# The last step of a layer norm moves from VectorE to ScalarE in an adjacency-attention kernel

## The chip, the cores and the metric

The kernel runs on one core of a Trainium2 chip. The metric is the device time of one launch in microseconds (us). Engine names in the profile: PE is TensorE, with PEld for its weight loads; DVE is VectorE; ACT is ScalarE; POOL is GpSimd; SP is SyncE, which issues the DMAs here. Each engine executes its own instructions strictly in the order in which the kernel lists them, and the engines are tied together by semaphores: an instruction may increment one when it has ended, and another engine waits for a value of it.

## What is computed

For each of 16 batches, with x of 1024 x 512 and an adjacency matrix of 1024 x 1024 that all batches share:

```python
q = jnp.einsum('bnd,ed->bne', neuron_states, Wq)
k = jnp.einsum('bnd,ed->bne', neuron_states, Wk)
v = jnp.einsum('bnd,ed->bne', neuron_states, Wv)
rel = jnp.einsum('bnd,bmd->bnm', q, k)
rel = adjacency.T[None, :, :] * rel
rel = rel / jnp.linalg.norm(rel, axis=2, keepdims=True)
return jnp.einsum('bnm,bmd->bnd', rel, v)
...
x = _layernorm(x + _L0_gnn_ref(x, adj, L0_gnn_Wq, L0_gnn_Wk, L0_gnn_Wv), axis=-1)
```

The layer norm is `(x - m) / sqrt(v + eps)`, with mean and variance over the 512 columns of a row, and no learned scale or bias.

## The kernel before

Every matrix product is made in three matmuls of split operands: each fp32 operand is split into a high part (a copy by ScalarE into a shorter format, names ending in `_hi`) and a low part (the difference, by VectorE or GpSimd, names ending in `_lo`), and `product` adds high by high, high by low and low by high (lines 339, 340 and 341). The products of the y and s stages are made by a Strassen-like scheme with seven products of blocks in place of eight.

A batch runs through four stages on TensorE, without a pause in between by its program:

- y stage (`y_products`): the batch's x by the combined weights. It makes 14 products of 6 matmuls in the order of `Y_ROUNDS` = 1, 5, 2, 6, 4, 7, 3, each round for j = 0 and 1. Round 2 adds onto the bank that round 1 filled, and so waits for `y_p1`, ScalarE's copy of round 1's result (line 495, the first thing that ScalarE does in a batch, for j = 0 and 1). Round 1 and round 5 make 24 matmuls together.
- s stage (`s_products`, two pairs of row blocks): 28 products that make `rel`. VectorE and GpSimd add the blocks and multiply them by the adjacency (line 669 is the first on VectorE), ScalarE squares them (line 534), GpSimd adds the squares (line 833) for the norm.
- v stage (`v_products`): eight products of 12 matmuls.
- output stage (`outputs`): eight tiles t of 128 rows, 24 matmuls each, into bank t. Tile t needs chunk t, the high and low parts of the 128 columns of `rel` that belong to it (`chunk_hi` by ScalarE, line 543; `chunk_lo` by VectorE, line 705). There are three chunk buffers (`CRING`), so chunk t+3 is made when tile t is done.

While TensorE makes the output tiles, the helpers do three things at once. For each t in turn, in this order:

- ScalarE makes `x_hi` of the next batch's x pieces (line 463; two pieces at t=0 and t=1, one at t=2 to 5, none at 6 and 7), then `chunk_hi` of t+3 once tile t is done. Nothing else stands in ScalarE's list there.
- VectorE makes `x_lo` of the same pieces (line 582, waits for `x_hi`), then `output(t)`: the sum of the scaled tile and the residual x (line 728), its statistics (731), mean and variance (733), and variance plus epsilon (735); then `chunk_lo` of t+3; then it waits for GpSimd's `rstd` and makes `normalise(t)` in place in `res`, tile (t mod 4) of a ring of four (line 740).
- GpSimd makes the sums of x pieces that the Strassen scheme wants (lines 780 to 792), S1 and S3 ahead of the first `power_var`, S2 ahead of the second, S4 ahead of the third; `power_var(t)` raises variance plus epsilon to the power -1/2 (line 850).
- SP stores tile t when `normed` counts it, and loads the residual for the ring's next use behind it (line 268). After the eighth tile it goes on to the next batch's four adjacency blocks (line 261).

At the end of the eight tiles every engine goes to the y stage of the next batch. The last batch has no next x to prepare. The first batch's x is prepared before the loop.

Of the kernel before, what the change touches and what calls it, by code (L numbers as in the profile page):

```python
# [5 lines left out]
F32 = mybir.dt.float32  # L6

F32R = mybir.dt.float32r
ALU = mybir.AluOpType
ACT = mybir.ActivationFunctionType  # L10
AX = mybir.AxisListType

P = 128
# [17 lines left out]
def adjacency_attention_layernorm(nc, x, xT, adj, wq, wk, wvT, a_kept, w_kept, out):  # L31
# [9 lines left out]
    MT = N // P  # L41
# [10 lines left out]
    RRING = 4  # L52

    with ExitStack() as ctx:
        def sb(name, shape, dt):
            return ctx.enter_context(nc.sbuf_tensor(name, shape, dt))

        def sem(name):
            return ctx.enter_context(nc.semaphore(name))
# [9 lines left out]
        res = sb("res", [P, RRING, D], F32)  # L69
# [7 lines left out]
        mean_var = sb("mean_var", [P, 2], F32)  # L77
        var_eps = sb("var_eps", [P, 1], F32)
        rstd = sb("rstd", [P, 1], F32)

        bank = [ctx.enter_context(nc.psum_tensor(f"bank{i}", [P, BANK], F32)) for i in range(8)]

# [65 lines left out]
        mean_var_made = sem("mean_var_made")  # L148
        var_made = sem("var_made")
        rstd_made = sem("rstd_made")  # L150
        normed = sem("normed")


# [53 lines left out]
        def v_bank(m):  # L207
            return bank[(2 + m) % 8]
# [44 lines left out]
        def cols(i):  # L253
            return slice(i * P, (i + 1) * P)
# [200 lines left out]
        def _(act):  # L455
            def x_piece(b, q):
                if q in (X22, X12):
                    act.wait_ge(x_loaded[1], b * DMA + DMA)
                elif q in (X21, X11):
                    act.wait_ge(x_loaded[0], b * DMA + DMA)  # L460
                else:
                    act.wait_ge(x_sum, b * 4 + x_sum_place[q])
                act.activation(x_hi[:, q, :, :], raw_of[q], ACT.Copy).then_inc(x_hi_made, 1)
# [28 lines left out]
            def y_blocks(b):  # L492
                for j in range(2):
                    act.wait_ge(y_done, y_count(b, 1, j))
                    act.activation(y_p1_raw[j], y_bank["a"][j][:], ACT.Copy).then_inc(y_p1, 1)
                for j in range(2):
                    act.wait_ge(y_done, y_count(b, 2, j))
                    act.activation(y_c11_raw[j], y_bank["a"][j][:], ACT.Copy).then_inc(y_c11, 1)
                    y_hi_piece(b, B11, j, y_bank["a"][j][:])
                for j in range(2):  # L500
                    act.wait_ge(y_done, y_count(b, 4, j))
                    y_hi_piece(b, T3, j, y_bank["b"][j][:])
                for j in range(2):
                    act.wait_ge(y_t2, b * 2 + (j + 1))
                    y_hi_piece(b, T2, j, y_t2_raw[j])
                for j in range(2):
                    act.wait_ge(y_c22, b * 2 + (j + 1))
                    y_hi_piece(b, B22, j, y_b22_raw[j])
                for j in range(2):
                    act.wait_ge(y_t1, b * 2 + (j + 1))  # L510
                    y_hi_piece(b, T1, j, y_t1_raw[j])
                    act.wait_ge(y_c12, b * 2 + (j + 1))
                    y_hi_piece(b, B21, j, y_b21_raw[j])

            def y_last_block(b):
                for j in range(2):
                    act.wait_ge(y_t4, b * 2 + (j + 1))
                    y_hi_piece(b, T4, j, y_t4_raw[j])

            def s_copy(b, i):  # L520
                act.wait_ge(s_done, s_count(b, 1, i))
                act.activation(c21(i), s_bank[i // 2]["a"][i % 2][:], ACT.Copy).then_inc(s_p1, 1)  # L522

            def square(b, name, i):
                act.wait_ge(masked_sem[name], b * HT + (i + 1))
                if (name, i) in firsts:

                    act.wait_ge(blocks_turned, b * HALVES + (half_of[name] + 1))
                    target = square_sum[:, half_of[name], :]
                else:  # L530
                    n = added_order.index((name, i))
                    act.wait_ge(square_added, b * ADDED + (n + 1))
                    target = squares[:, n % SQRING, :]
                act.activation(target, block_of[name](i), ACT.Square).then_inc(squared, 1)  # L534

            def chunk(b, t):
                if t < CRING:
                    act.wait_ge(s_done, b * S_COUNT + S_COUNT)
                    for masked in (s_m11, s_m22, s_m21, s_m12):
                        act.wait_ge(masked, b * HT + HT)  # L540
                else:
                    act.wait_ge(o_done, b * MT + (t - CRING + 1))
                act.activation(chunk_hi[t % CRING], rel[:, :, cols(t)], ACT.Copy).then_inc(chunk_hi_made, 1)  # L543

            def v_piece(b, m):
                act.wait_ge(v_done, b * MT + (m + 1))
                act.activation(v_hi[:, m, :], v_bank(m)[:], ACT.Copy).then_inc(v_hi_made, 1)

            def batch(b, last):
                y_blocks(b)  # L550
                s_copy(b, 0)
                s_copy(b, 1)
                y_last_block(b)
                for name, i in square_order[0:6]:
                    square(b, name, i)
                s_copy(b, 2)
                s_copy(b, 3)
                for name, i in square_order[6:]:
                    square(b, name, i)
                for m in range(MT):  # L560
                    v_piece(b, m)
                    if m in (1, 2):
                        chunk(b, m - 1)
                chunk(b, 2)
                if not last:
                    act.wait_ge(v_done, b * MT + MT)
                for t in range(MT):
                    if not last:
                        for q in {0: (X22, X21), 1: (X11, X12), 2: (S1,), 3: (S3,), 4: (S2,), 5: (S4,)}.get(t, ()):
                            x_piece(b + 1, q)  # L570
                    if t + CRING < MT:
                        chunk(b, t + CRING)

            with act.Fori(0, B - 1) as b:
                batch(b, False)
# [3 lines left out]
        def _(dve):  # L579
            def x_piece(b, q):  # L580
                dve.wait_ge(x_hi_made, b * 8 + x_place[q])
                dve.tensor_tensor(x_lo[:, q, :, :], raw_of[q], x_hi[:, q, :, :].bitcast(F32),  # L582
                                  ALU.subtract).then_inc(x_split, 1)
# [114 lines left out]
            def v_piece(b, m):  # L698
                dve.wait_ge(v_hi_made, b * MT + (m + 1))
                dve.tensor_tensor(v_lo[:, m, :], v_bank(m)[:], v_hi[:, m, :].bitcast(F32),  # L700
                                  ALU.subtract).then_inc(v_split, 1)

            def chunk(b, t):
                dve.wait_ge(chunk_hi_made, b * MT + (t + 1))
                dve.tensor_tensor(chunk_lo[t % CRING], rel[:, :, cols(t)], chunk_hi[t % CRING].bitcast(F32),
                                  ALU.subtract).then_inc(chunk_split, 1)
# [27 lines left out]
                dve.wait_ge(mean_var_made, b * MT + (t + 1))  # L734
                dve.tensor_scalar(var_eps[:, :], mean_var[:, 1:2], EPS, None, ALU.add).then_inc(var_made, 1)  # L735

            def normalise(b, t):
                slot = t % RRING
                dve.wait_ge(rstd_made, b * MT + (t + 1))
                dve.tensor_scalar(res[:, slot, :], res[:, slot, :], mean_var[:, 0:1], rstd[:, 0:1],  # L740
                                  ALU.subtract, ALU.mult).then_inc(normed, 1)

            def batch(b, last):
                y_blocks(b)
                s_blocks(b, 0)
                s_blocks(b, 1)
                for m in range(MT):
                    v_piece(b, m)
                    if m in (1, 2):
                        chunk(b, m - 1)  # L750
                    if m == 3:
                        norms(b)
                chunk(b, 2)
                for t in range(MT):
                    if not last:
                        for q in {0: (X22, X21), 1: (X11, X12), 2: (S1,), 3: (S3,), 4: (S2,), 5: (S4,)}.get(t, ()):
                            x_piece(b + 1, q)
                    output(b, t)
                    if t + CRING < MT:
                        chunk(b, t + CRING)  # L760
                    normalise(b, t)

            with dve.Fori(0, B - 1) as b:
                batch(b, False)
# [3 lines left out]
        def _(pool):  # L768
# [78 lines left out]

            def power_var(b, t):
                pool.wait_ge(var_made, b * MT + (t + 1))
                pool.tensor_tensor(rstd[:, :], var_eps[:, :], minus_half[:, 0:1], ALU.pow).then_inc(rstd_made, 1)  # L850

            def batch(b, last):
# [43 lines left out]
```

## Time and profile before

| | |
|---|---|
| median of 3 runs | 2037.12 us (2036.22 to 2037.63) |
| the profiled execution | 2035.14 us, its span 2033.0 us |
| PE, busy share of the span | 98% |
| PEld | 80% |
| DVE | 73% |
| POOL | 46% |
| ACT | 34% |
| line 740 (normalise), DVE | 128 instructions, 100.9 us, mean 788 ns |
| its idle time before, ended by line 850 on POOL | 102.7 us, 128 times |
| mean granted TensorE clock | 0.994 |

The span runs from the first to the last instruction; the rest of the profiled execution's time lies around it. Busy shares are means over the whole span and over stages with different limits. Matmuls are pipelined: each is shown with about 0.39 us, and in an undisturbed stretch one starts every 0.227 us. In the timelines the time in brackets is the engine's idle time before the instruction and the work that ended it.

### The profile page before, as it was taken

The numbers are of one execution on the slowest core, as the hardware profiler recorded it, in microseconds if no ns is written. First come the engines' busy times: TensorE is split into PE (matmuls) and PEld (weight loads), VectorE is DVE, ScalarE is ACT, GpSimd is POOL, SyncE is SP. The second block draws the span as 40 slices with busy tenths as digits, with TensorE's granted clock in tenths as the row PEclk, the third lists the DMA queues.
The fourth block names the chain that finished last, engine by engine and source line by source line (L and its number), as shares of the span: only waits on it lengthen the run. The fifth ranks groups of instructions, "written<-read, shape, count | busy, mean of one in ns | idle before, by whom it ended". The sixth has DMA issues, their size and how long they took to land.

```text
span 2033.0 us, 26047 instructions
## 1 busy us (share of the span) xinstructions
PE 1983.2 (98%) x8688; PEld 1631.2 (80%) x8688; DVE 1484.1 (73%) x2199; ACT 701.2 (34%) x1016; POOL 927.2 (46%) x629
## 2 busy tenths in 40 slices
PE   4999999999999999999999999999999999999998
PEld 3787887878878787887878878788787888878787
DVE  6777777776777677676777777777787677767765
ACT  5342423333233332333423234242333323333331
POOL 2643437344363453535535364353734536355351
PEclk7999999999999999999999999999999999999999
DMA  6344342334333334233342424333333332333401
GB/s 240 122 161 139 139 140 103 129 132 157 124 118 126 132 139 160 83 143 115 150 150 101 155 87 157 139 149 130 113 124 134 150 132 111 129 129 139 160 21 62
DMA packets 70443, 265.44 MB, mean 131 GB/s; under 512 B 7328, under 2 KB 7328, under 8 KB 66208
## 3 DMA queue, kind: packets, MB, share of 16 engines
q1 hardware_dynamic: 70432, 265.32, 35.9%
q8 instruction: 4, 0.07, 0.0%
q14 instruction: 7, 0.06, 0.0%
HBM read 225.97 MB, written 39.32 MB: 130 GB/s over the span
## 4 chain that ended last, share of the span: by engine, by line
PE 87%; DVE 8%; ACT 2%; issue 2%; DMA 0%; SPq 0%; DVEq 0%; POOLq 0%; POOL 0%; ACTq 0%
PE bank L339 29%; PE bank L341 29%; PE bank L340 29%; DVE yv L619 5%; ACT yv L490 2%; DVE rel L640 1%; DVE rel L654 0%; DVE rel L647 0%; DMA scr<-xT 0%; DVE x_lo L582 0%; ACT rel L522 0%; DVE aw L605 0%; DVE rel L598 0%; DVE rel L595 0%; DVE rel L596 0%
## 5 line engine op out<-in xcount | busy, mean ns | idle before, releaser
L339 PE MATMUL bank<-yv 128*128 128x512 f32 x1024 | 398.3, 389 | 0.0
L340 PE MATMUL bank<-yv 128*128 128x512 f32 x1024 | 398.3, 389 | 0.0
L341 PE MATMUL bank<-yv 128*128 128x512 f32 x1024 | 398.3, 389 | 0.0
L339 PE MATMUL bank<-yv,x_hi 128*128 128x512 f32 x896 | 351.5, 392 | 18.5 <-DVE yv L619 16.8
L833 POOL TENSOR_TENSOR square_sum<-square_sum,squares 128x512 f32<-128x512 f32 x224 | 319.2, 1425 | 103.8 <-ACT squares L534 93.3
L340 PE MATMUL bank<-yv,x_hi 128*128 128x512 f32 x896 | 348.9, 389 | 0.0
L341 PE MATMUL bank<-yv,x_lo 128*128 128x512 f32 x896 | 348.8, 389 | 0.0
L850 POOL TENSOR_TENSOR rstd<-var_eps,minus_half 128x1 f32<-128x1 f32 x128 | 130.7, 1021 | 335.5 <-DVE var_eps L735 335.5
L534 ACT ACTIVATE squares<-rel 128x512 f32<-128x512 f32 x224 | 140.1, 632 | 282.2 <-POOL rel L826 99.4
L341 PEld LDWEIGHTS bank<-yv 128*128 128x128 f32 x1024 | 192.2, 188 | 40.0
L340 PEld LDWEIGHTS bank<-yv 128*128 128x128 f32 x1024 | 192.2, 188 | 39.9
L339 PEld LDWEIGHTS bank<-yv 128*128 128x128 f32 x1024 | 192.2, 188 | 39.8
L339 PEld LDWEIGHTS bank<-yv,x_hi 128*128 128x128 f32 x896 | 168.1, 188 | 65.5 <-issue 31.5
L543 ACT ACTIVATE yv<-rel 128x1024 fp32r<-128x1024 f32 x128 | 135.5, 1059 | 243.0 <-PE bank L341 243.0
L339 PE MATMUL bank<-aw,x_hi 128*128 128x512 f32 x512 | 199.2, 389 | 0.0
L340 PE MATMUL bank<-aw,x_hi 128*128 128x512 f32 x512 | 199.2, 389 | 0.0
L341 PE MATMUL bank<-aw,x_lo 128*128 128x512 f32 x512 | 199.2, 389 | 0.0
L341 PEld LDWEIGHTS bank<-yv,x_lo 128*128 128x128 f32 x896 | 168.2, 188 | 35.1
L340 PEld LDWEIGHTS bank<-yv,x_hi 128*128 128x128 f32 x896 | 168.2, 188 | 34.0
L339 PE MATMUL bank<-x_hi,aw 128*128 128x512 f32 x448 | 175.2, 391 | 19.1 <-DVE yv L611 19.1
L740 DVE TENSOR_SCALAR res<-res,mean_var,rstd 128x512 f32<-128x512 f32 x128 | 100.9, 788 | 102.7 <-POOL rstd L850 102.7
L340 PE MATMUL bank<-x_lo,aw 128*128 128x512 f32 x448 | 175.0, 391 | 0.0
(75 smaller groups left out, 3108.9 us busy)
## 6 DMA issues: line engine op xcount, KB each, us to landing
scr<-adj SPq DMA_DIRECT2D x128, 512.0 KB, 5.5
aw<-a_kept SPq DMA_DIRECT2D x15, 3584.0 KB, 11.2
scr<-xT SPq DMA_DIRECT2D x32, 1024.0 KB, 6.8
res<-x SPq DMA_DIRECT2D x128, 256.0 KB, 2.7
aw<-w_kept SPq DMA_DIRECT2D x16, 2048.0 KB, 8.0
out<-res SPq DMA_DIRECT2D x128, 256.0 KB, 2.0
a_kept<-aw SPq DMA_DIRECT2D x1, 3584.0 KB, 16.4
w_kept<-yv SPq DMA_DIRECT2D x1, 2048.0 KB, 6.3
```

The lines of the kernel that those rows point to most:

```text
L339: pe.matmul(bank_ap, l_hi, r_hi, start=first and i == 0, stop=False, skip_group_check=on)
L340: pe.matmul(bank_ap, l_hi, r_lo, start=False, stop=False, skip_group_check=on)
L341: mm = pe.matmul(bank_ap, l_lo, r_hi, start=False, stop=i == len(pairs) - 1, skip_group_check=on)
L490: act.activation(y_hi[:, q, j, :], source, ACT.Copy).then_inc(y_hi_made[q], 1)
L534: act.activation(target, block_of[name](i), ACT.Square).then_inc(squared, 1)
L543: act.activation(chunk_hi[t % CRING], rel[:, :, cols(t)], ACT.Copy).then_inc(chunk_hi_made, 1)
L619: dve.tensor_tensor(y_lo[:, q, j, :], source, y_hi[:, q, j, :].bitcast(F32), ALU.subtract).then_inc(y_split[q], 1)
L640: dve.tensor_tensor(y_t2_raw[j], bb[j][:], y_c11_raw[j], ALU.add).then_inc(y_t2, 1)
L740: dve.tensor_scalar(res[:, slot, :], res[:, slot, :], mean_var[:, 0:1], rstd[:, 0:1], ALU.subtract, ALU.mult).then_inc(normed, 1)
L833: pool.tensor_tensor(square_sum[:, h, :], square_sum[:, h, :], squares[:, n % SQRING, :], ALU.add).then_inc(square_added, 1)
L850: pool.tensor_tensor(rstd[:, :], var_eps[:, :], minus_half[:, 0:1], ALU.pow).then_inc(rstd_made, 1)
```

## The change

The step that subtracts the mean and multiplies by `rstd` goes from VectorE to ScalarE, as one activation: identity of `rstd * res + shift`. VectorE makes the column `shift` = -mean * rstd in its place, where normalise stood, after the same wait for `rstd`. ScalarE's normalise(t) stands at the end of tile t in its list, behind the x pieces of t and chunk t+3, and waits for `shift`. SP's store waits for `normed` as before, which ScalarE now increments. GpSimd's `power_var(t)` gets one more wait, for normalise(t-1), since ScalarE may still read the one `rstd` column.

```diff
--- before.py
+++ after.py
@@ -77,6 +77,7 @@
         mean_var = sb("mean_var", [P, 2], F32)
         var_eps = sb("var_eps", [P, 1], F32)
         rstd = sb("rstd", [P, 1], F32)
+        shift = sb("shift", [P, 1], F32)
 
         bank = [ctx.enter_context(nc.psum_tensor(f"bank{i}", [P, BANK], F32)) for i in range(8)]
 
@@ -148,6 +149,7 @@
         mean_var_made = sem("mean_var_made")
         var_made = sem("var_made")
         rstd_made = sem("rstd_made")
+        shift_made = sem("shift_made")
         normed = sem("normed")
 
 
@@ -546,6 +548,12 @@
                 act.wait_ge(v_done, b * MT + (m + 1))
                 act.activation(v_hi[:, m, :], v_bank(m)[:], ACT.Copy).then_inc(v_hi_made, 1)
 
+            def normalise(b, t):
+                slot = t % RRING
+                act.wait_ge(shift_made, b * MT + (t + 1))
+                act.activation(res[:, slot, :], res[:, slot, :], ACT.Identity, bias=shift[:, 0:1],
+                               scale=rstd[:, 0:1]).then_inc(normed, 1)
+
             def batch(b, last):
                 y_blocks(b)
                 s_copy(b, 0)
@@ -570,6 +578,7 @@
                             x_piece(b + 1, q)
                     if t + CRING < MT:
                         chunk(b, t + CRING)
+                    normalise(b, t)
 
             with act.Fori(0, B - 1) as b:
                 batch(b, False)
@@ -734,11 +743,11 @@
                 dve.wait_ge(mean_var_made, b * MT + (t + 1))
                 dve.tensor_scalar(var_eps[:, :], mean_var[:, 1:2], EPS, None, ALU.add).then_inc(var_made, 1)
 
-            def normalise(b, t):
-                slot = t % RRING
+            def make_shift(b, t):
+
                 dve.wait_ge(rstd_made, b * MT + (t + 1))
-                dve.tensor_scalar(res[:, slot, :], res[:, slot, :], mean_var[:, 0:1], rstd[:, 0:1],
-                                  ALU.subtract, ALU.mult).then_inc(normed, 1)
+                dve.tensor_scalar(shift[:, :], mean_var[:, 0:1], rstd[:, 0:1], -1.0,
+                                  ALU.mult, ALU.mult).then_inc(shift_made, 1)
 
             def batch(b, last):
                 y_blocks(b)
@@ -758,7 +767,7 @@
                     output(b, t)
                     if t + CRING < MT:
                         chunk(b, t + CRING)
-                    normalise(b, t)
+                    make_shift(b, t)
 
             with dve.Fori(0, B - 1) as b:
                 batch(b, False)
@@ -847,6 +856,9 @@
 
             def power_var(b, t):
                 pool.wait_ge(var_made, b * MT + (t + 1))
+
+                if t > 0:
+                    pool.wait_ge(normed, b * MT + t)
                 pool.tensor_tensor(rstd[:, :], var_eps[:, :], minus_half[:, 0:1], ALU.pow).then_inc(rstd_made, 1)
 
             def batch(b, last):
```

## Rows read from the trace of the kernel before

**Rows 1.** The page, part 1: busy us (share of the span) xinstructions.

```profile
PE 1983.2 (98%) x8688; PEld 1631.2 (80%) x8688; DVE 1484.1 (73%) x2199; ACT 701.2 (34%) x1016; POOL 927.2 (46%) x629
```

**Rows 2.** Waits of PE, whole run: us in total, times, longest us.

```profile
PE bank L339 <- DVE yv L611: 19.1, 1, 19.1
PE bank L339 <- DVE yv L619: 16.8, 16, 1.1
```

**Rows 3.** Busy time by stretch: stretch, length, engines' busy us, PEclk, DMA share, GB/s.

```profile
1034.00:1062.00 28.00, 26.85 (x118) 21.62 (x117) 20.23 (x28) 11.38 (x20) 10.70 (x8) 1.00 0.55 197
```

**Rows 4.** Timeline of PE, 1028 to 1062: start us, us, instruction, idle before.

```profile
1034.11 0.39 PE L339 MATMUL bank<-x_hi,aw 128*128 128x512 f32 x1
...
1039.55 0.39 PE L339 MATMUL bank<-x_hi,aw 128*128 128x512 f32 x1
...
1060.17 0.49 PE L339 MATMUL bank<-yv,x_hi 128*128 128x512 f32 x1 [1.05 <-DVE yv L619]
```

**Rows 5.** Timeline of DVE, 1002 to 1062.

```profile
1002.25 0.55 DVE L740 TENSOR_SCALAR res<-res,mean_var,rstd 128x512 f32<-128x512 f32 x1 [2.80 <-POOL rstd L850]
1002.71 2.36 DVE L582 TENSOR_TENSOR x_lo<-scr,x_hi 128x1024 fp32r<-128x1024 f32 x2
...
1008.85 2.61 DVE L740 TENSOR_SCALAR res<-res,mean_var,rstd 128x512 f32<-128x512 f32 x1 [0.45 <-POOL rstd L850]
...
1016.46 1.22 DVE L582 TENSOR_TENSOR x_lo<-scr,x_hi 128x1024 fp32r<-128x1024 f32 x1
1017.60 0.75 DVE L728 SCALAR_TENSOR_TENSOR res<-bank,rnorm,res 128x512 f32<-128x512 f32 x1
...
1019.43 1.22 DVE L705 TENSOR_TENSOR yv<-rel,yv 128x1024 fp32r<-128x1024 f32 x1
1021.10 0.55 DVE L740 TENSOR_SCALAR res<-res,mean_var,rstd 128x512 f32<-128x512 f32 x1 [0.44 <-POOL rstd L850]
...
1027.78 0.74 DVE L728 SCALAR_TENSOR_TENSOR res<-bank,rnorm,res 128x512 f32<-128x512 f32 x1
...
1030.36 0.55 DVE L740 TENSOR_SCALAR res<-res,mean_var,rstd 128x512 f32<-128x512 f32 x1 [0.66 <-POOL rstd L850]
...
1034.41 0.75 DVE L728 SCALAR_TENSOR_TENSOR res<-bank,rnorm,res 128x512 f32<-128x512 f32 x1 [0.46 <-PE bank L341]
...
1056.69 3.35 DVE L619 TENSOR_TENSOR yv<-rel,yv 128x512 fp32r<-128x512 f32 x2
...
1061.86 0.69 DVE L669 TENSOR_TENSOR rel<-bank,scr 128x512 f32<-128x512 f32 x1 [0.62 <-PE bank L341]
```

**Rows 6.** Timeline of ACT, 996 to 1036.

```profile
997.21 1.99 ACT L463 ACTIVATE x_hi<-scr 128x1024 fp32r<-128x1024 f32 x2
...
1002.64 1.04 ACT L463 ACTIVATE x_hi<-scr 128x1024 fp32r<-128x1024 f32 x1
...
1035.67 0.60 ACT L495 ACTIVATE rel<-bank 128x512 f32<-128x512 f32 x1 [15.67 <-PE bank L341]
```

**Rows 7.** Groups by line, whole run: count, busy us, mean ns, idle before.

```profile
L534 ACT ACTIVATE squares<-rel 128x512 f32<-128x512 f32 x224 | 140.1, 632 | 282.2 <-POOL rel L826 99.4 <-DVE rel L669 74.5 <-DVE rel L688 72.6
...
L728 DVE SCALAR_TENSOR_TENSOR res<-bank,rnorm,res 128x512 f32<-128x512 f32 x128 | 95.5, 746 | 28.1 <-PE bank L341 28.1
...
L684 DVE TENSOR_TENSOR rel<-bank,rel 128x512 f32<-128x512 f32 x64 | 44.3, 692 | 42.6 <-PE bank L341 42.6
...
L735 DVE TENSOR_SCALAR var_eps<-mean_var 128x1 f32<-128x1 f32 x128 | 19.7, 154 | 4.4
...
L467 ACT ACT_TABLE_LOAD x1 | 1.3, 1283 | 0.7 <-PEq L887 0.7
```

**Rows 8.** Timeline of POOL, 1001 to 1036.

```profile
1001.66 0.55 POOL L850 TENSOR_TENSOR rstd<-var_eps,minus_half 128x1 f32<-128x1 f32 x1
...
1008.78 2.39 POOL L792 TENSOR_TENSOR scr<-scr 128x1024 f32<-128x1024 f32 x1
```

**Rows 9.** Timeline of SP's DMA queue, 1036 to 1064.

```profile
1040.58 1.75 SPq L261 DMA_DIRECT2D scr<-adj  x4
```

## The prediction

> **What bounds the kernel now.** I read the busy times first, then the waits of TensorE, then the timeline engine by engine around one edge between two batches. TensorE is busy 98% of the span [rows 1]. In the whole run it waits twice while the weights are prepared (the longer one is shown) and after that in one place alone, once in each of the 16 batches, 1.05 us for a low part in the y stage [rows 2]. So less work on VectorE can give back at most 16.8 us, and only if it shortens that wait; everything else VectorE does is cover. In the other direction each microsecond by which a helper is too late for TensorE is paid in full, 15 or 16 times. The question is therefore how much slack the helpers have where the change touches them: in the output stage (eight tiles t = 0 to 7) and at the edge to the next batch. The clock is at its upper level of 2.4 GHz there, granted 1.00 in a stretch that has one of those waits [rows 3].
>
> The rows are of the eighth batch; the other edges repeat them. The next batch's first TensorE instruction starts at 1034.11 and the first that needs y_p1 (k=2) at 1039.55, 24 matmuls or 5.44 us later [rows 4]. An output tile has 24 matmuls too, so TensorE makes one every 5.44 us. VectorE needs 0.46 + 1.14 + 3.50 = 5.1 us for a tile that also splits a piece of the next batch's x (the three terms are taken below), so it just keeps up, and at t=7 it is waiting for TensorE (1034.41 [rows 5]). ScalarE has 15.67 us of idle time before its first work of the next batch [rows 6]. That looks like room for eight more instructions, but it is not idle time in the place where the new ones stand.
>
> **The change part by part.** Removed from VectorE: normalise, 0.55 us each, one of 2.61 in each batch but the last [rows 5]. Added to VectorE: make_shift on one column. The nearest row is the sum of variance and epsilon on one column, 0.154; reading a column as operand adds 0.054 by the pair of forms of 128x512 from PSUM, 0.746 with one against 0.692 without [rows 7]; two columns give 0.262. I take the middle, 0.21, with 0.154 and 0.262 as ends.
>
> Added to ScalarE: one activation of 128x512 with two columns. The trace has none. The same function costs 0.55 on VectorE [rows 5], the lower end. Square, same shape, SBUF to SBUF, takes 0.632 [rows 7]; two columns at 0.054 make 0.74, which I take, since it is this engine and this shape. Upper end: the 0.746 row plus one more column, 0.80. Of this, 0.09 overlaps the next instruction (two of 1.04 in 1.99 [rows 6]), so it occupies 0.65. The Trainium skill, "ScalarE: Activation LUTs", What ACT_TABLE_LOAD costs, gives 186 ns plus 0.833 ns an element with immediates and some 93 ns for each column operand; that makes an estimate of 0.80 us, and by it the loss worked out below would be 4.1 us a batch and the time about 2099. No run here shows a column operand on ScalarE so far.
>
> Moved: the step's place in ScalarE's order. ScalarE executes for each t: pieces of x_hi for the next batch, the chunk t+3, then normalise(t). Behind normalise(t), which waits for VectorE's shift(t), which waits for GpSimd's power, now stand the x_hi pieces of t+1, and VectorE's first instruction of tile t+1 (x_lo) waits for just those. Before, ScalarE made that piece while VectorE was still in tile t (x_hi at 1002.64, behind a chunk that waits only for TensorE [rows 6]). This is the new wait; queued behind it are all of VectorE's tile t+1, and with it chunk_lo, power and store.
>
> One link of that loop, from the start S of shift(t): shift 0.21, handoff 0.04 (power ends 1001.66 + 0.55 = 1002.21, its waiter starts 1002.25 [rows 5, 8]), normalise 0.65, x_hi 1.04, handoff 0.04: x_lo starts at S + 1.98. Before it started 0.46 after the start of normalise (1002.25 to 1002.71). Then x_lo to the residual sum 1.14 (1016.46 to 1017.60), and from there to the next shift 3.50 with a chunk (1017.60 to 1021.10), 2.58 without (1027.78 to 1030.36) [rows 5]. A link is 1.98 + 1.14 + 3.50 = 6.62 us, against TensorE's 5.44: VectorE now falls behind by 1.2 us a tile.
>
> The chain at this edge, in times of the trace before. S0 = 1002.25, set by GpSimd's sums and unchanged. x_lo 1004.23, 1.52 late, so S1 = 1008.85 + 1.52 = 1010.37. The next x_lo could start at 1012.35. But GpSimd's last x sum, which before began at 1008.78 [rows 8], now runs 1010.30 to 1012.69, and VectorE's normalise that began 0.07 after it before took 2.61 instead of 0.55: one held up the other. The removal takes that stall away; I let x_lo wait for the end of the sum instead, 1012.69 (0.34 less a batch, 5 us in all, if it need not). The Trainium skill, "SBUF — State Buffer", SBUF: two separate sides, tells of a port pair of VectorE and GpSimd that one of them locks for a whole instruction; by that rule x_lo waits as I let it, and the 2.61 agrees. S2 = 1012.69 + 1.14 + 3.50 = 1017.33, S3 = 1023.95, S4 = 1030.57. x_lo 1032.55, sum 1033.69, S5 = 1036.27. Tiles 6 and 7 have no x piece, so no ScalarE in the loop: 0.12 for the shift (0.21 less an overlap of 0.09, as 0.55 took 0.46) + 2.58 each: S6 = 1038.97, S7 = 1041.67. The last normalise starts at 1041.92; y_p1, behind it on ScalarE, at 1042.57, ends 0.60 later at 1043.17 [rows 6]. TensorE starts 0.13 after what it waited for (1056.69 + 3.35 = 1060.04 to 1060.17 [rows 4, 5]): 1043.30 in place of 1039.55. **Loss 3.75 us a batch.**
>
> Part of it comes earlier: the chunk_lo of t+3 ends 1.83 + 1.22 us after the sum of t [rows 5]. Those of 6 and 7 end at 1023.50 and 1030.12, and TensorE wants them at 1023.23 and 1028.67 (1034.11 less 10.88 and 5.44). It stops there for 0.4 and 1.2 us, and for the remaining 2.2 us at y_p1. These are parts of the 3.75, not on top of it: once TensorE is late by them, y_p1 is wanted that much later. After y_p1 the helpers wait for TensorE again, so nothing carries to the next edge.
>
> Hidden: GpSimd's new wait for normalise(t-1) holds power(t) and the x sums queued behind. Normalise(5) ends at 1037.26 and power(6) has its input at 1038.4; for t=1 the margin is over 5 us; if it failed, it would add its own lateness to the link. SP's store(7) goes out about 5 us later, and behind it the reloads and the next batch's four adjacency loads (1040.58, 1.75 us of issues [rows 9]): at the latest 1047.4, their first reader is at 1061.86 [rows 5] and moves 3.75 later itself. The 14 us left cost nothing unless the transfers take longer than that. In the last batch there are no x pieces, so no lag; its end gets 0.21 + 0.04 + 0.74 in place of 0.55, 0.4 us.
>
> **The sum.** 15 edges by 3.75 is 56.3, plus 0.4: 56.7. The profiled execution took 2035.14, so 2091.8; it lies 2.0 below the median of the runs, 2037.12, so **2094**. With the low ends (0.55 and 0.154) the loss is 2.4 a batch, 2074; without the hold-up by the sum as well, 2069. With the high ends (0.80 and 0.262), 4.4 and 2104; six handoffs to ScalarE, each bounded by one row of another engine, I allow another 0.4 for, 2110.
>
> **The rivals.** *No change:* ScalarE's extra work stays under cover. Place: y_p1. It decides if y_p1 starts by 1039.55 - 0.13 - 0.60 = 1038.82. With VectorE level with TensorE at t=7 it would (sum 1034.41, shift 1036.99, y_p1 1037.89). So it needs the five links to shed 3.75 us, 0.75 each, as if x_hi were still made ahead. For it: ScalarE's 15.67 idle and VectorE 0.34 us lighter a tile. Against it: program order puts x_hi behind normalise. Then 2037.5; chance 0.05. *Faster:* VectorE's relief (128 times 0.34) reaches the one wait [rows 2] and removes it, 2020. Against it: that wait ends 22 us behind the last normalise (1037.55 to 1060.17), and ScalarE, which comes in between, begins with a wait for TensorE [rows 6]. 0.02. *Table loads:* Identity is not in the loaded table, and each normalise costs two loads of 1.283 [rows 7] on ScalarE. Five links, and once more ahead of y_p1, by 2.57 is 15.4 a batch on top: about 2325. For it: nothing; the trace has one load with Copy and Square both in use. The Trainium skill, "ScalarE: Activation LUTs", Table sets, says that cheap functions, identity and copy among them, are in every set; the single load agrees as far as it goes. 0.03.
>
> **How the numbers follow.** The loop through ScalarE: 0.90, at 2094. The 0.10 of the rivals lies outside 2069 to 2110, and I leave 0.10 for lags that I mis-sized, so the range stays there. About 0.2% (4 us) is what a measurement of this kernel can tell from no change: faster 0.02, same 0.05, slower 0.93.
>
> **What would show it.** TensorE waiting some 15 times each for chunk_lo of tiles 6 and 7 (line of chunk on VectorE) and 15 times some 2 us for ScalarE's y_p1; VectorE waiting five times a batch for ScalarE's x_hi, where x_lo now follows normalise directly; tile spacing near 6.6 us for t=2 to 4; the last batch's output stage unchanged. Wrong would be: normalise far from 0.74, x_lo not waiting for x_hi, a second kind of table load, or a granted clock below 1.00 around the new stops, which I left at no cost.

## The result

| | us |
|---|---|
| before, median of 4 runs | 2036.67 |
| changed, median of 4 runs (2117.75 to 2121.16) | 2119.53 |
| ratio, 95% interval | 1.0407, 1.0389 to 1.0425 |
| forecast, range | 2094, 2069 to 2110 |
| the profiled execution of the changed kernel, its span | 2119.11, 2117.0 |

The direction and the place were right, the size was not: 83 us instead of 57. Line numbers of the changed kernel are 2 to 12 higher: matmuls 341 to 343, y_p1 497, x_hi 465, x_lo 591, chunk_lo 714, shift 749, normalise 554.

First the waits of TensorE in the changed kernel, for the whole run (us in total, times, the longest):

```profile
PE bank L341 <- ACT rel L497: 30.0, 15, 2.0
PE bank L341 <- DVE yv L620: 20.4, 1, 20.4
PE bank L341 <- DVE yv L628: 16.8, 16, 1.1
PE bank L341 <- DVE yv L714: 16.7, 30, 1.0
```

Beside [rows 2], the wait for a low part of y (line 628) is the same 16.8. Two are new: 15 for ScalarE's y_p1, 2.00 us each, and 30 for chunk_lo. Together they are 46.7 us, not 83.

VectorE's timeline at the edge that [rows 5] show (start us, us, instruction, idle before). All times of this execution are 38.62 us later there (1040.87 against 1002.25):

```profile
1040.87 0.21 DVE L749 TENSOR_SCALAR shift<-mean_var,rstd 128x1 f32<-128x1 f32 x1 [2.80 <-POOL rstd L862]
1042.91 2.36 DVE L591 TENSOR_TENSOR x_lo<-scr,x_hi 128x1024 fp32r<-128x1024 f32 x2 [1.83 <-ACT x_hi L465]
...
1055.89 0.21 DVE L749 TENSOR_SCALAR shift<-mean_var,rstd 128x1 f32<-128x1 f32 x1 [0.44 <-POOL rstd L862]
1057.94 1.23 DVE L591 TENSOR_TENSOR x_lo<-scr,x_hi 128x1024 fp32r<-128x1024 f32 x1 [1.83 <-ACT x_hi L465]
...
1062.58 0.21 DVE L749 TENSOR_SCALAR shift<-mean_var,rstd 128x1 f32<-128x1 f32 x1 [0.44 <-POOL rstd L862]
1064.62 1.23 DVE L591 TENSOR_TENSOR x_lo<-scr,x_hi 128x1024 fp32r<-128x1024 f32 x1 [1.83 <-ACT x_hi L465]
...
1080.44 0.21 DVE L749 TENSOR_SCALAR shift<-mean_var,rstd 128x1 f32<-128x1 f32 x1 [0.66 <-POOL rstd L862]
```

ScalarE's timeline at the same edge, beside [rows 6]:

```profile
1056.14 0.81 ACT L554 ACTIVATE res<-res,shift,rstd 128x512 f32<-128x512 f32 x1 [4.11 <-DVE shift L749]
1056.86 1.05 ACT L465 ACTIVATE x_hi<-scr 128x1024 fp32r<-128x1024 f32 x1
...
1080.69 0.81 ACT L554 ACTIVATE res<-res,shift,rstd 128x512 f32<-128x512 f32 x1 [1.89 <-DVE shift L749]
1081.41 1.06 ACT L497 ACTIVATE rel<-bank 128x512 f32<-128x512 f32 x2
```

x_lo waits 1.83 us for x_hi in tiles 1 to 5, all that have one but tile 0; x_hi stands behind normalise, normalise behind shift. Tiles follow each other by 1062.58 - 1055.89 = 6.69 us, against TensorE's 5.44. The last normalise starts at 1080.69 and y_p1 at 1081.41.

TensorE's timeline at the same edge: the stops for the chunks of tiles 6 and 7, the first instruction of the y stage, and the stop at y_p1:

```profile
1062.19 0.50 PE L341 MATMUL bank<-yv 128*128 128x512 f32 x1 [0.17 <-DVE yv L714]
...
1068.87 0.50 PE L341 MATMUL bank<-yv 128*128 128x512 f32 x1 [0.91 <-DVE yv L714]
...
1074.44 0.39 PE L341 MATMUL bank<-x_hi,aw 128*128 128x512 f32 x1
...
1079.65 0.39 PE L343 MATMUL bank<-x_hi,aw 128*128 128x512 f32 x1
1082.04 0.76 PE L341 MATMUL bank<-x_hi,aw 128*128 128x512 f32 x1 [2.00 <-ACT rel L497]
1082.60 0.63 PE L342 MATMUL bank<-x_lo,aw 128*128 128x512 f32 x1
1083.03 0.63 PE L343 MATMUL bank<-x_hi,aw 128*128 128x512 f32 x1
...
1085.56 0.39 PE L343 MATMUL bank<-x_hi,aw 128*128 128x512 f32 x1
1085.80 0.40 PE L341 MATMUL bank<-x_hi,aw 128*128 128x512 f32 x1
```

The last matmul before the stop starts at 1079.65. Behind it they start some 0.43 us apart instead of 0.227, and at the old pace again from 1085.56 on. The busy time by stretch (length, busy us of PE, PEld, DVE, ACT, POOL, then the granted clock, DMA share, GB/s) shows the same as the granted clock, at 0.53 and 0.62 in two stretches where [rows 3] had 1.00; its two levels, 1.2 and 2.4 GHz, are mixed in them:

```profile
1072.00:1078.00 6.00, 6.00 (x28) 4.99 (x27) 4.39 (x12) 0.83 (x2) 1.10 (x2) 1.00 0.31 91
...
1082.00:1084.00 2.00, 1.96 (x5) 1.57 (x6) 1.29 (x2) 0.48 (x1) 0.00 (x0) 0.53 0.63 232
1084.00:1086.00 2.00, 2.00 (x7) 1.58 (x6) 0.00 (x0) 1.03 (x2) 0.00 (x0) 0.62 0.68 169
...
1088.00:1092.00 4.00, 4.00 (x20) 3.30 (x19) 2.29 (x4) 0.60 (x1) 0.00 (x0) 1.00 0.86 323
```

That is a third loss which stands in no wait: the nine steps from 1082.04 to 1085.80 take 3.76 us instead of 9 x 0.227 = 2.04.

### The profile page after: what moved, and what is told of

It is laid out like the page before. It is cut to its first block, busy times and chain, and to the rows that moved or that the text cites. A ratio compares the mean times of both kernels' runs of the same rounds, so it can differ in the third digit from the quotient of the medians.

```text
span 2117.0 us, 26287 instructions
## 1 busy us (share of the span) xinstructions
PE 2018.9 (95%) x8688; PEld 1644.2 (78%) x8688; DVE 1416.9 (67%) x2199; ACT 795.5 (38%) x1144; POOL 927.3 (44%) x629
## 4 chain that ended last, share of the span: by engine, by line
issue 37%; PE 26%; POOL 17%; DVE 10%; ACT 7%; POOLq 1%; DMA 0%; SPq 0%; ACTq 0%; DVEq 0%
PE bank L341 9%; PE bank L342 9%; PE bank L343 9%; POOL square_sum L842 7%; POOL rstd L862 5%; DVE yv L628 5%; ACT res L554 4%; ACT yv L492 2%; POOL scr L789 2%; POOL rel L835 1%; DVE x_lo L591 1%; POOL rnorm L855 1%; DVE shift L749 1%; DVE rel L649 1%; POOL scr L801 1%
## 5 line engine op out<-in xcount | busy, mean ns | idle before, releaser
L341 PE MATMUL bank<-yv,x_hi 128*128 128x512 f32 x896 | 351.6, 392 | 18.5 <-DVE yv L628 16.8
L554 ACT ACTIVATE res<-res,shift,rstd 128x512 f32<-128x512 f32 x128 | 104.4, 816 | 470.5 <-DVE shift L749 470.5
L591 DVE TENSOR_TENSOR x_lo<-scr,x_hi 128x1024 fp32r<-128x1024 f32 x128 | 158.1, 1257 | 140.5 <-ACT x_hi L465 140.5
L341 PE MATMUL bank<-x_hi,aw 128*128 128x512 f32 x448 | 187.4, 418 | 50.3 <-ACT rel L497 30.0
L342 PE MATMUL bank<-x_lo,aw 128*128 128x512 f32 x448 | 184.5, 412 | 0.0
```

The costliest lines, as they stand in the source:

```text
L341: pe.matmul(bank_ap, l_hi, r_hi, start=first and i == 0, stop=False, skip_group_check=on)
L342: pe.matmul(bank_ap, l_hi, r_lo, start=False, stop=False, skip_group_check=on)
L554: act.activation(res[:, slot, :], res[:, slot, :], ACT.Identity, bias=shift[:, 0:1], scale=rstd[:, 0:1]).then_inc(normed, 1)
```

## The experiments

The theory: VectorE falls behind by its loop through ScalarE; TensorE pays for that at the chunks and at y_p1; and the stop at y_p1 brings its clock down. The rivals: the new instruction on ScalarE is itself too much work, or in the way of y_p1 wherever it stands; the slow matmuls have another cause.

**Is it the order or the instruction?** ScalarE makes the x pieces of t+1 ahead of normalise(t); all else is as in the changed kernel.

```diff
-                for t in range(MT):
+                def x_pieces(t):
                     if not last:
                         for q in {0: (X22, X21), 1: (X11, X12), 2: (S1,), 3: (S3,), 4: (S2,), 5: (S4,)}.get(t, ()):
                             x_piece(b + 1, q)
+
+                x_pieces(0)
+                for t in range(MT):
                     if t + CRING < MT:
                         chunk(b, t + CRING)
+                    x_pieces(t + 1)
                     normalise(b, t)
```

> The changed kernel, but ScalarE makes the x_hi pieces of tile t+1 before normalise(t), so that VectorE's x_lo no longer stands behind normalise. Theory (the loop shift - normalise - x_hi - x_lo makes VectorE late): VectorE needs 5.10 - 0.34 = 4.8 us a tile again, is level with TensorE at t=7, y_p1 on ScalarE starts about 1.5 us before TensorE wants it, no new stops, 2037 (2035 to 2040). Rival (the normalise of 0.82 us on ScalarE is itself too much, or it holds up y_p1 wherever it stands): the stop ahead of k=2 stays and the time is above 2080.

Measured: 2037.09, ratio 1.0003 (0.9994 to 1.0013). TensorE's waits, with both new ones gone (line numbers shift by a few from run to run):

```profile
PE bank L341 <- DVE yv L624: 20.8, 1, 20.8
PE bank L341 <- DVE yv L632: 16.8, 16, 1.1
```

And ScalarE and VectorE at the same place, where all times of that run are 0.95 later than in [rows 5]:

```profile
1003.45 0.82 ACT L554 ACTIVATE res<-res,shift,rstd 128x512 f32<-128x512 f32 x1 [3.30 <-DVE shift L753]
...
1038.20 0.82 ACT L554 ACTIVATE res<-res,shift,rstd 128x512 f32<-128x512 f32 x1 [4.62 <-DVE shift L753]
1038.93 1.06 ACT L497 ACTIVATE rel<-bank 128x512 f32<-128x512 f32 x2
```

```profile
1009.47 0.21 DVE L753 TENSOR_SCALAR shift<-mean_var,rstd 128x1 f32<-128x1 f32 x1 [0.44 <-POOL rstd L866]
1009.60 3.29 DVE L595 TENSOR_TENSOR x_lo<-scr,x_hi 128x1024 fp32r<-128x1024 f32 x1
```

Normalise still takes 0.82 us, 128 times; y_p1 starts at 1038.93, behind it, and was wanted 0.84 later (1038.82 + 0.95 = 1039.77). So the instruction, its engine and its place ahead of y_p1 cost nothing that can be measured; the order against x_hi cost all 83 us. The last line answers the 2.61 of normalise in [rows 5]: GpSimd's sum, which runs from 1009.40 to 1011.80 in this trace, now holds up x_lo instead, 3.29 us for 1.22. The hold-up moved to the next instruction. In the changed kernel x_lo came later, near the end of the sum, and took 1.37.

**Which tiles?** The change for a part of the tiles, with the rest on VectorE as before. Only ScalarE's part of the edit is shown; VectorE's branch and the semaphores of the two sets are left out here.

```diff
-                    normalise(b, t)
+                    if t in ON_ACT:
+                        normalise(b, t)
```

With `ON_ACT` = 0 to 4:

> Only tiles 0 to 4 are normalised on ScalarE, tiles 5 to 7 on VectorE as before. VectorE falls behind as in the changed kernel, but nothing stands in front of y_p1 on ScalarE. Theory: the two stops for chunk_lo of tiles 6 and 7 stay, some 1.5 us an edge, the stop ahead of k=2 is gone, and with it the fall of the granted clock: 2037 + 15 x 1.5 = 2060. Rival (any of the new stops brings the clock down): 1.7 us an edge more, 2085. Rival (the lag alone is what counts, wherever TensorE meets it): about 2120 as in the changed kernel.

Measured: 2061.79, ratio 1.0124 (1.0107 to 1.0141). With `ON_ACT` = 5 to 7:

> Only tiles 5 to 7 are normalised on ScalarE; none of them has x pieces of a next tile behind it. Theory: no lag, VectorE level with TensorE at t=7, y_p1 behind the last normalise starts about 1.5 us early enough: 2037. Rival (y_p1 is late because normalise(7) stands in front of it, not because of the lag): a stop of 2 us at each of 15 edges with the clock's fall, 2085 or more.

Measured: 2037.45, ratio 1.0003 (0.9994 to 1.0013). The waits of TensorE with tiles 0 to 4 on ScalarE:

```profile
PE bank L349 <- DVE yv L637: 16.8, 16, 1.1
PE bank L349 <- DVE yv L723: 16.3, 30, 1.0
```

The first five make the lag, and TensorE's two chunk stops with it, 30 times as in the changed kernel; the wait for y_p1 is gone, since ScalarE is free by then, and the clock stayed at 1.00. (2061.79 - 2036.71) / 15 = 1.67 us an edge. The last three make no lag and cost nothing, though normalise(7) stands in front of y_p1.

**Do the slow matmuls come from the stop?** The changed kernel, with 8 matmuls of no use to the result, where TensorE would stand still.

```diff
                     pe.wait_ge(x_split, b * 8 + x_place[left])
+                    if k == 2:
+                        pe.wait_ge(o_taken, b * MT + (4 + 0 + 1))
+                        for n in range(8):
+                            pe.matmul(y_bank["c"][0][:], a_hi[:, right, 0, cols(0)], x_hi[:, left, 0, :],
+                                      start=True, stop=True)
```

> The changed kernel with 8 more matmuls on TensorE, of no use to the result, ahead of the wait for y_p1 (k=2, j=0); at the 15 edges they run in the 2 us in which TensorE stood still there, in the first batch they cost 8 x 0.227 = 1.8 us. Theory (the ten matmuls behind the stop at 0.43 us apart are the granted clock's fall, brought by the stop): the clock stays at 1.00, 1.7 us an edge less than the changed kernel, 2119.5 - 26 + 2 = 2095. Rival (the slow matmuls have another cause, such as ScalarE's copies at that time): nothing gained, 2120 to 2122.

Measured: 2098.77, ratio 1.0306 (1.0288 to 1.0323): 20.8 us less than the changed kernel, with more work. Its mean granted clock is 0.994, as before, against 0.983. Of the wait for y_p1 1.7 us are left:

```profile
PE bank L341 <- DVE yv L719: 16.3, 30, 0.9
...
PE bank L341 <- ACT rel L502: 1.7, 10, 0.2
```

So the slow matmuls do come from the stop. One run with a timing of its own could have missed them by luck, as the runs below show; but in none of the twelve traces does TensorE, once the first batch is done, go over to 0.43 us a matmul anywhere except behind a stop of 1.78 us or more. The time is 4 us above the 2095 that were expected, most of it because that sum took a fall of 1.72 us at all 15 edges: there were 14, and 0.14 us of each comes behind any stop, so 14 x 1.58 = 22 us were to be had, not 26. The rest is the first batch, where the added matmuls cost more than the 1.8 us allowed for: its v stage starts at 103.91 for 100.89 in the changed kernel.

**What stop brings the clock down?** In the kernel before, y_p1 of j=0 is made N times over on ScalarE, so that TensorE stops at k=2 and nowhere else.

```diff
                     act.wait_ge(y_done, y_count(b, 1, j))
+                    if j == 0:
+                        for n in range(N):
+                            act.activation(y_p1_raw[j], y_bank["a"][j][:], ACT.Copy).then_inc(copied, 1)
+                            act.wait_ge(copied, b * N + (n + 1))
```

N = 7:

> The kernel before, with y_p1 of j=0 made eight times over on ScalarE in each batch (each of the 7 extra copies waits for the one before; some 0.64 us each, 4.5 in all). y_p1 had 1039.42 - 1036.27 = 3.15 us to spare, so TensorE starts k=2 some 1.3 us late, in all 16 batches, with nothing else changed: 2037 + 16 x 1.3 = 2058. Theory (the clock falls for a stop of 2 us, not for one of about 1): granted clock 1.00 behind these stops. Rival (the clock falls for any stop at this place): 1.7 us a batch more, 2085.

Measured: 2062.14, ratio 1.0125 (1.0108 to 1.0141). N = 8:

> As the run with 7 extra copies, with 8: y_p1 5.1 us later, TensorE starts k=2 some 2.0 us late in 16 batches, one stop alone, without the two stops for chunks ahead of it. Theory (a stop of 2 us at k=2 brings the clock down by itself, 1.7 us each time): 2037 + 16 x (2.0 + 1.7) = 2096. Rival (it takes the changed kernel's chunk stops as well): the stop alone, 2069.

Measured: 2071.77, ratio 1.0173 (1.0156 to 1.0190). The stops were 1.02 and 1.65 us, not 1.3 and 2.0, and behind none of the 15 later ones in either run did the matmuls slow down. (The first batch stops for longer in these runs and lost its clock there; it is left out of the counts.) With N = 7 that is what the theory said, for stops at this one spacing. With N = 8 the stop came out too short to compare: the time is close to the rival's, but a stop of 1.65 us is not one of 2.0. One more run has a stop as long as the changed kernel's, with N = 8 and a copy of half the columns:

> As the run with 8 extra copies (stop of 1.65 us at k=2, no fall of the clock behind 15 of 16), plus one copy of half the columns, some 0.4 us: one stop of 2.05 us, as long as the changed kernel's 2.00, without chunk stops ahead of it. Theory (a stop of 2.0 us brings the clock down by itself in most batches): (2071.8 - 2036.3) + 16 x 0.4 + 14 x 1.6 = 64 over the kernel before, 2101. Rival (it takes the chunk stops as well): the stop alone, 42 over, 2078, and matmuls 0.227 apart behind it.

Measured: 2080.89, ratio 1.0217 (1.0200 to 1.0234). The stop was 2.07 us, and the clock fell behind one of 15. So the theory that a stop of 2 us is enough does not hold; nor does the rival quite, since one did fall without chunk stops. Two runs then changed only when the stops come, by 5 matmuls of no use to the result at the start of the v stage:

```diff
+                    if m == 0:
+                        for n in range(5):
+                            pe.matmul(v_bank(m)[:], x_hi[:, X11, 0, cols(0)], wv_hi[:, 0, :], start=True, stop=True)
```

In the last one above:

> The run with one stop of 2.07 us (8 and a half extra copies; its clock fell behind 1 of 15 later stops), with 5 matmuls of no use to the result at the start of the v stage, far from the stop: each batch 5 x 0.227 = 1.13 us longer, the stop itself unchanged. Theory (whether the clock falls is a matter of when a stop of this size comes, so of the time between stops): the fall comes behind a different number of the 15 stops, several at least, 2080.9 + 18 + 1.6 for each fall more. Rival (without the chunk stops ahead of it a stop of 2 us is too short): again at most 2 of 15, 2099.

Measured: 2113.77, ratio 1.0377 (1.0360 to 1.0395). In the changed kernel:

> The changed kernel (stop of 2.00 us at k=2, clock fell behind 14 of 15) with the same 5 extra matmuls at the start of the v stage, 1.13 us a batch. Theory (when the stop comes decides): the falls no longer come in nearly every batch, several of 15 go, 2119.5 + 18 less 1.6 for each. Rival (the stop with its chunk stops always brings it down): 14 or 15 of 15, 2137.5.

Measured: 2122.50, ratio 1.0420 (1.0403 to 1.0438). With the counts of the next table the two expectations come to 2115 (10 falls more) and 2123 (9 fewer).

The stops and what followed, from TensorE's timeline at each of the 15 edges:

| run | stop at k=2, us | chunk stops ahead | edges with slow matmuls behind it |
|---|---|---|---|
| changed kernel | 2.00 | yes | 14 |
| the same, 5 matmuls more in the v stage | 1.95 to 2.00 | yes | 5 |
| one column in normalise (below) | 1.78 to 1.82 | yes, one | 10 |
| 8 extra copies and a half | 2.07 | no | 1 |
| the same, 5 matmuls more in the v stage | 2.07 | no | 11 |
| 8 extra copies | 1.65 | no | 0 |
| 7 extra copies | 1.02 | no | 0 |

Two stops of the same run, 8 and a half copies with the 5 matmuls, the first followed by slow matmuls and the second not (stretches of 10 us by engine, as above):

```profile
565.00:575.00 10.00, 7.93 (x28) 6.12 (x27) 3.27 (x5) 5.14 (x10) 0.00 (x0) 0.83 0.76 262
824.00:834.00 10.00, 7.93 (x36) 6.51 (x36) 3.99 (x7) 5.24 (x10) 0.00 (x0) 1.00 0.71 257
```

The two stops are as long as each other, and PE is busy for the same 7.93 us in both stretches; the granted clock is 0.83 in one and 1.00 in the other. In this run the slow matmuls begin at the stop's end or up to six matmuls behind it, so the fall is not tied to the first matmul either. The 5 matmuls lie far from the stop and changed it by 0.05 us at most, but took the count from 1 to 11 in one kernel and from 14 to 5 in the other. So for stops of this size it is when the stop comes that decides, not its length alone and not the chunk stops ahead. The stops of 1.65 and 1.02 us were tried at one spacing each, so their 0 of 15 do not show that such a stop is safe at every spacing. What the time is counted against is not shown by any run here. The Trainium skill, "TensorE: Matmul & The Clock Gate", What's actually happening, has the clock gated by a monitor whose view of TensorE's activity runs on freely and does not start anew with the kernel; the two counts agree with that.

**The price of a column.** The changed kernel with the scale column alone; this kernel leaves out the mean's subtraction.

```diff
-                act.activation(res[:, slot, :], res[:, slot, :], ACT.Identity, bias=shift[:, 0:1],
-                               scale=rstd[:, 0:1]).then_inc(normed, 1)
+                act.activation(res[:, slot, :], res[:, slot, :], ACT.Copy,
+                               scale=rstd[:, 0:1]).then_inc(normed, 1)
```

> The changed kernel with ScalarE's normalise as a copy with the scale column alone; the shift is made and waited for, but not added (the mean's subtraction is left out). It prices one column operand on ScalarE and the slope of the loop. If each column costs 0.09 (0.816 with two against 0.632 for Square): normalise 0.72, each of six passes 0.09 shorter, TensorE 0.5 us an edge less late, 2119.5 - 8 = 2111; less by up to 25 more if the stop ahead of k=2 then no longer brings the clock down. If the columns cost nothing and Identity is slow: normalise stays near 0.63 or 0.82 whatever the columns.

Measured: 2106.14, ratio 1.0340 (1.0323 to 1.0357). Groups by line (count, busy us, mean ns, idle before), the changed kernel first, then this one:

```profile
L554 ACT ACTIVATE res<-res,shift,rstd 128x512 f32<-128x512 f32 x128 | 104.4, 816 | 470.5 <-DVE shift L749 470.5
...
L749 DVE TENSOR_SCALAR shift<-mean_var,rstd 128x1 f32<-128x1 f32 x128 | 27.4, 214 | 102.6 <-POOL rstd L862 102.6
```

```profile
L554 ACT ACTIVATE res<-res,rstd 128x512 f32<-128x512 f32 x128 | 92.6, 724 | 474.9 <-DVE shift L749 474.9
```

0.632 for Square [rows 7], 0.724 for Copy with one column, 0.816 for Identity with two: 0.092 each. The function is not what costs: Copy without a column, same shape, SBUF to SBUF, takes 0.628 in the changed kernel (line 492). The Trainium skill, "ScalarE: Activation LUTs", What ACT_TABLE_LOAD costs, gives some 93 ns for each, and the runs agree. The clock fell at 4 edges fewer, 6.4 us of the 13.4 gained; the rest is a shorter loop.

## Why the prediction was wrong

**Right:** the loop and its place. The starts of shift(1) to shift(7), less 38.62, were 1010.44, 1017.27, 1023.96, 1030.64, 1036.41, 1039.12 and 1041.82, each within 0.15 us of the working. TensorE started k=2 at 1082.04 - 38.62 = 1043.42, forecast 1043.30: 3.87 us late in place of 3.75. Of that, 1.71 came by the two chunk stops (1074.44 - 38.62 = 1035.82 for 1034.11; 1.6 forecast) and 2.16 at y_p1 (2.2 forecast). Shift measured 0.214, as taken; normalise 0.816 instead of 0.74, just above the 0.80 that was its upper end; 0.07 more in each link, which the wait behind GpSimd's sum at t=2 partly took up. The three rivals are out: no table load but the first, no gain, no cover. One reading was off without touching the sum: TensorE's wait of 1.05 us is for a low part of y, but falls in the s stage, 7 us behind its start (1053.15 to 1060.17).

**Wrong:** the price of nothing on the granted clock. The working rested on [rows 3], where the clock stayed at 1.00 with a stop of 1.05 us, and forecast a stop of 2.2 us at y_p1, twice that, without a price; it stood among the things that would make the prediction wrong, without a chance and without a place in the range. It came as forecast (2.00 of idle time), and behind 14 of 15 the clock fell, for 1.72 us, of which 0.14 comes behind every such stop; 1.6 net.

**The sum as measured**, on the spans: 15 x 3.87 = 58.1 for the late start of k=2; 14 x 1.6 = 22.4 for the clock; 15 x 0.14 = 2.1; 0.8 in the first batch, which differs from run to run (its v stage starts at 100.89 for 100.06); 0.5 at the end (0.4 forecast). Together 83.9; the spans differ by 2117.0 - 2033.0 = 84.0. The clock is the large term that the forecast's sum lacked: with it, the forecast would have been 2094 + 22 = 2116, against 2119.5 measured. What is left is small: 0.12 us more an edge, and the 0.14.

**The relief** was worth nothing, as forecast: VectorE's busy time fell from 1484 to 1417 us, and with the order mended the time is the one of before.

## What to carry to other kernels

An instruction that moves to an idle engine takes a place in that engine's order, and all that it waits for then stands in front of what is queued behind it: look there, not at the busy shares, and put work made ahead for the next step in front of it. A stop of TensorE of 2 us may cost 1.6 us more than itself in clock, so a sum that creates such stops needs that term, or at least an end of the range with it. An experiment on the clock wants several stops and a second period between them, since one count can be 1 of 15 or 11 of 15 for the same stop.

## What had not been expected of the hardware

Stops of TensorE of 1.0 and 1.65 us brought its clock down in none of 30 cases (one spacing each), stops of 1.8 to 2.07 did so in 41 of 75 cases, depending on when they came; each fall slowed eight or so matmuls from 0.227 to 0.43 us apart. Filling a stop with 8 useless matmuls made the kernel 20.8 us faster. The 2.06 us by which GpSimd's sum held up VectorE's normalise went to VectorE's next large instruction when normalise left and that instruction followed at once; where it came 1.83 us later, 0.15 us of them were left.
